# One carried-rows step over four PSUM banks in place of two over two, with new order tables

## The reference, cut to what matters

```python
u = layernorm(x)
zxbcdt = u @ W_in.T                       # z0 512, x0 512, (512 unused), xBC 544, dt 8
dt  = softplus(dt + dt_bias);  A = -exp(A_log)
x, B, C = split(silu(conv4(xBC) + conv_b))       # 8 heads of 64 channels, state of 16
for each token t, each head:                     # the scan
    h = exp(dt_t * A) * h + dt_t * x_t * B_t
    y_t = h . C_t + D * x_t
y = layernorm(y) * ln_gamma + ln_beta
y = sigmoid(y @ W_gate.T + b_gate) * y
x = x + concat(silu(z0) * x0, y) @ W_out.T
# feed-forward
h = layernorm(gelu(layernorm(x) @ ternary(W_fc).T)) ; x = x + h @ ternary(W_proj).T
```

## Time and profile before

| what | value |
|---|---|
| median of three runs | 1161.18 us |
| the profiled execution | 1162.07 us |
| its span (first to last instruction) | 1160.3 us |
| granted TensorE clock, mean | 0.990 |
| PE busy | 1102.1 us, 95% |
| ACT busy | 978.0 us, 84% |
| DVE busy | 969.4 us, 84% |
| POOL busy | 381.9 us, 33% |
| L494, the carried rows | 512 records, 34.2 us |

### The profile page before, as it was taken

How to read it: one execution, slowest core, us unless ns; L and a number is a source line. 1 busy time by engine, 2 the same in 40 slices (tenths; PEclk the granted TensorE clock), 3 DMA queues, 4 the chain that set the end, 5 groups by cost and what they waited for, 6 DMA issues and landing times. The chain is left out here.

```text
span 1160.3 us, 23258 instructions
## 1 busy us (share of the span) xinstructions
PE 1102.1 (95%) x8534; PEld 716.8 (62%) x8534; DVE 969.4 (84%) x1958; ACT 978.0 (84%) x1694; POOL 381.9 (33%) x500
## 2 busy tenths in 40 slices
PE   3789999999999999999999999999999999999995
PEld 1455756576675666666576675756667566757663
DVE  5999999788788898878979898788889889586654
ACT  5787789989888999989798898789888987888765
POOL 1122315341532435142340533323342242515431
PEclk9899999999999999999999999999999999999999
DMA  6510222242424325243424324324343142332465
GB/s 197 165 47 20 66 56 40 57 91 56 93 55 82 85 39 116 47 92 74 72 58 89 68 65 92 84 41 92 77 85 76 37 93 55 74 56 55 89 112 127
DMA packets 238978, 89.15 MB, mean 77 GB/s; under 512 B 207761, under 2 KB 235153, under 8 KB 238865
## 3 DMA queue, kind: packets, MB, share of 16 engines
q1 hardware_dynamic: 238864, 87.67, 35.2%
HBM read 24.32 MB, written 8.39 MB: 28 GB/s over the span
## 5 line engine op out<-in xcount | busy, mean ns | idle before, releaser
L359 PE MATMUL bank<-xnT,win 128*128 128x512 f16 (+1 forms) x1248 | 299.5, 386 | 23.3 <-DMA xnT<-hb 20.3
L359 PEld LDWEIGHTS bank<-xnT,win 128*128 128x128 f16 (+1 forms) x1248 | 121.7, 101 | 156.4 <-issue 31.4
L947 DVE SCALAR_TENSOR_TENSOR cv<-bank,cws,cv 128x510 f32<-128x510 f32 (+5 forms) x240 | 177.8, 744 | 8.3 <-ACT tail L676 2.0
L180 ACT ACT_TABLE_LOAD x137 | 175.8, 1283 | 2.4
L359 PE MATMUL bank<-yhl,wg 128*128 128x512 f16 x768 | 171.6, 379 | 0.5 <-DVE yhl L1094 0.4
L1212 POOL TENSOR_TENSOR cat<-sz,cat 128x512 f16<-128x512 f32 x64 | 78.5, 1229 | 277.6 <-ACT cat L784 277.6
L1208 POOL TENSOR_TENSOR caty<-tg,caty 128x512 f16<-128x512 f32 x64 | 85.5, 1343 | 147.8 <-ACT caty L770 147.8
L587 PE MATMUL bank<-wpj,hT 128*128 128x256 f16 x1024 | 122.6, 274 | 10.3 <-DMA hT<-hb 10.2
L359 PEld LDWEIGHTS bank<-yhl,wg 128*128 128x128 f16 x768 | 74.1, 98 | 89.9 <-issue 2.6
L575 PE MATMUL bank<-wfc,x3T 128*128 128x512 f16 x512 | 122.2, 379 | 3.4 <-ACT EM L741 1.5
L587 PEld LDWEIGHTS bank<-wpj,hT 128*128 128x128 f16 x1024 | 99.2, 98 | 32.3 <-issue 11.5
(11 more groups left out here) (146 smaller groups left out, 2056.3 us busy)
## 6 DMA issues: line engine op xcount, KB each, us to landing
x<-in_x SPq DMA_DIRECT2D x32, 512.0 KB, 4.2
out_y<-x SPq DMA_DIRECT2D x15, 512.0 KB, 3.2
crep<-cv SPq DMA_DIRECT2D x128, 32.0 KB, 2.0
hT<-hb SPq DMA_TRANSPOSE x128, 3.2
caty<-in_wg SPq DMA_DIRECT2D x1, 1024.0 KB, 7.2
x<-in_wout SPq DMA_DIRECT2D x1, 1024.0 KB, 7.2
hT<-in_wfc SPq DMA_DIRECT2D x1, 1024.0 KB, 6.8
cat<-in_wpj SPq DMA_DIRECT2D x1, 1024.0 KB, 8.9
```

Source lines behind the costliest of these rows:

```text
L180: self.eng.preload_act_table_set(self.table)
L359: m = eng.matmul(b, lhs(p, k), rhs(q, k), start=(n == 0), stop=(n == len(seq) - 1))
L947: op = eng.scalar_tensor_tensor(cs[0:w, j, 3 - k:T], b[0:w, 0:T - 3 + k], cws[0:w, j, k:k + 1], cs[0:w, j, 3 - k:T], ALU.mult, ALU.add)
```

## The change

`carried` is now one step a block. It takes four banks at once, and for each chunk gives the products of all four head pairs one after the other, each in its own 32 rows of the array and in its own bank: 16 products in one step, 16 steps in the kernel, where there were 32 steps of 8. `own` and `y_rows` find their banks in the one list. Three waits on the carried step's semaphore count to `i` in place of `2 * i`. The products, their operands and their number are the same.

All five order tables are new. `PE_ORDER` has 980 words in place of 996; the others have as many as before, in another order. Line numbers after `PE_ORDER` go down by one or two.

```diff
 PE_ORDER = (
-    "... q747 q712 o56 p44 ... q717 q720 r735 w7 w7 f56 G64 G61 f57 f52 r704 w7 w7 p41 f53 ..."
+    "... G61 G66 q775 r74312 q760 w7 w7 G67 p45 G66 f50 w7 w7 v77 f56 y75 ..."
...
-            def carried(i, half, at0, at1):
-                js = ((2 * half, at0), (2 * half + 1, at1))
-                hold = {j: take(at) for j, at in js}
+            def carried(i, n, *at):
+                hold = [take(b) for b in at]
                 pe.wait_ge(ce, i + 1)
                 pe.wait_ge(s_done, i + 1)
                 for c in range(NCH):
-                    for j, _ in js:
+                    for j in range(4):
                         m = eng.matmul(hold[j][:, chunk(c)], S[32 * j:32 * j + 32, (4 * i + c) % 5, :],
                                        ec[32 * j:32 * j + 32, chunk(c)], start=(c == 0), stop=False,
                                        skip_group_check=True)
                 m.then_inc(car_mm, 1)
-                for j, at in js:
-                    gives(at, y_out, 4 * i + j + 1)
+                for j in range(4):
+                    gives(at[j], y_out, 4 * i + j + 1)
 
             def own(i, n):
                 p, half = UNITS[n]
-                hold = bank["r", i, half]
+                hold = bank["r", i, 0]
                 pe.wait_ge(em, 4 * i + n + 1)
                 for c in (2 * p, 2 * p + 1):
-                    for j in (0, 1):
+                    for j in (2 * half, 2 * half + 1):
                         for e in range(2):
-                            at = (2 * half + j) * P + 64 * e
+                            at = j * P + 64 * e
...
-                act.wait_ge(car_mm, 2 * i)
+                act.wait_ge(car_mm, i)
...
-                                         bank["r", i, half][j % 2][:, :], ALU.mult, ALU.add).then_inc(y_out, 1)
+                                         bank["r", i, 0][j][:, :], ALU.mult, ALU.add).then_inc(y_out, 1)
```

More of the change, by code:

```diff
@@ L497, in carried @@
                 m.then_inc(car_mm, 1)
-                for j, at in js:
-                    gives(at, y_out, 4 * i + j + 1)
+                for j in range(4):
+                    gives(at[j], y_out, 4 * i + j + 1)
             def own(i, n):
                 p, half = UNITS[n]
-                hold = bank["r", i, half]
+                hold = bank["r", i, 0]
                 pe.wait_ge(em, 4 * i + n + 1)
                 for c in (2 * p, 2 * p + 1):
-                    for j in (0, 1):
+                    for j in (2 * half, 2 * half + 1):
                         for e in range(2):
-                            at = (2 * half + j) * P + 64 * e
+                            at = j * P + 64 * e
                             m = eng.matmul(hold[j][64 * e:64 * e + 64, chunk(c)], Xd[:, c, at:at + 64],
-                                           EM[:, c % 2, 4 * (n % 2) + 2 * j + e, :], start=False, stop=True,
+                                           EM[:, c % 2, 4 * (n % 2) + 2 * (j % 2) + e, :], start=False, stop=True,
                                            skip_group_check=True)
@@ L1014, in zero_s @@
             def zero_s(i, n):
-                dve.wait_ge(car_mm, 2 * i)
+                dve.wait_ge(car_mm, i)
                 then(eng.memset(S[:, (4 * i) % 5, :], 0.0))
```

## The result

The changed kernel takes **1157.15 us** (median of 9 runs, 1155.89 to 1158.96); the kernel before takes 1161.18 (9 runs beside them). The ratio is 0.996, 95% interval 0.9947 to 0.9974: 4 to 5 us faster (3 to 6 by the interval). The forecast was 1150, some 11 us faster. The direction was right, the size somewhat over a third of what I had said.

What follows compares the result with a forecast made beforehand. The prediction took PE's work to bound the middle 900 us: 1162.1 − 13.0 saved + 1.5 of new waits = 1150.6, so 1150 us for a median. The forecast case spanned 1145 to 1155, the whole range 1141 to 1165.

Steps and rivals of the forecast that it cites:

- What the change takes from PE: Carried step: one four-bank step takes 1.16 us and the second step of each block goes, saving 13.0 us.
- the 15 that I had set as its limit: Sign of a right forecast: PE's idle time in the middle 900 us stays under 15 us.
- The first rival: Carried step: four row groups do not run together, pairs go one after the other; 1158 us, chance 0.06.
- the first paragraph: What bounds the kernel: PE, busy 887.53 of the middle 900 us, so PE work removed there shortens the span unless waits replace it.
- the whole term of 13.0 us: Carried steps: PE time saved, 9 x 1.05 us for separate blocks plus 6 x 0.6 us for blocks with halves together.
- I take back 1.5 us: PE in the middle: allowance for new waits for banks, an eighth of the 12.5 us idle, bounds nothing to 15.6 us.
- My second rival: Carried steps: one bank wait of 1.04 us in 15 blocks, 15.6 us, against the 13.0 gained; 1164 us, chance 0.12.
- The remaining reordering: Rest of the new order tables: costed at nothing, with a bound of 5 us either way.
- The fourth rival: New tables: waits such as block 3's go and the ends shorten by a few microseconds; 1142 us, chance 0.10.

Runs made afterwards that it cites:

- (2): Changed kernel with its new tables, each four-bank carried step put back as two two-bank steps side by side: 1157.53 us, ratio 0.9963 to the kernel before.
- (1): Kernel before with its own tables, each carried step leaving out the last two of its four chunks, nothing moved: 1163.27 us, ratio 1.0007.
- (5): Kernel before with 14 of the 16 products in every projection step: 1166.02 us, ratio 1.0031.
- (13): Kernel before with 8 of 16 projection and 2 of 4 fc products: 1156.18 us; its companions, ACT work cut 1152.86 us, DVE work cut 1148.73 us.
- (3): Kernel before with its old tables, the two carried steps joined into one four-bank step in ten of sixteen blocks: 1167.15 us, ratio 1.0038.
- tables_four: Changed kernel's steps (four-bank carried step) with all five order tables re-made, words moved and banks renamed: 1191.12 us, ratio 1.0248 to the kernel before.
- tables_two: Kernel before's two two-bank carried steps with tables re-made in the same way, starting from its own: 1188.0 us, ratio 1.0219.

## Why the prediction was right in direction by luck, and wrong in size and cause

*What the change takes from PE: right.* Four row groups run side by side, the step takes 1.17 us for my 1.16, the group 19.7 us for 18.6 (17 to 19 was the range I gave). PE's busy time fell by 10.2 and not 15: the carried group fell by 14.5, and the other groups together grew by 4.3. PE's idle time in the middle, 16.0 us, came out just above the 15 that I had set as its limit. The first rival is out. The rule of the Trainium skill in "TensorE: Matmul & The Clock Gate", section "Part 3: Packing small matmuls — row/col tiling", which I had weighed as 0.3 us more a block, does not show: four row groups of 128 columns cost no more than two did. The skill's figure is for 512 columns, which no run here has for four row groups.

*The failed step is the first paragraph: "in the middle every microsecond of PE work that goes is a microsecond of the span, unless a wait takes its place".* It carried the whole term of 13.0 us, and that term is worth nothing: the new tables take the same time with one step of four banks and with two of two banks, within about 2 us (2). The same saving in the old tables gave nothing (1), 14 us at the projection made the kernel 3.6 us slower (5), and 116 us gave 6 (13). I had read 98.6% busy as "PE sets the end" and 12.5 us of idle time as all the room there was.

So the right direction was luck. The 4 to 5 us come from the term that I had put at nothing, the new order, and not from the one that I had forecast.

Why did the row mislead? In part since PE's busy time can hold waits. PE's group of projection products in the changed kernel:

```profile
L585 PE MATMUL bank<-wpj,hT 128*128 128x256 f16 x1024 | 122.8, 276 | 10.8 <-DMA hT<-hb 10.3 <-ACT ec L724 0.4
```

Each record lasts 276 ns, but 122.8 us over 1024 of them is 120 ns from one to the next: they overlap. So after the last product of a step some 0.15 us go by before PE counts as idle. I counted from start to start, over the usual distance of each form. By that estimate the 900 us in the middle of the kernel before hold some 110 us beyond the products, of which about 80 us are some 800 gaps of 0.06 to 0.3 us, mostly where one step gives way to the next; the view shows 12.5 us. The level depends on what is taken as a form's need: over the fastest step of each kind it is 46 us. How much of it is waiting and how much a cost of changing over I cannot say. When the products went in experiment 1, this sum rose by 7 to 11 us, and in experiment 13 by 70 to 85 us, whichever way it is counted.

The other part is not in any view of one engine: PE, ACT and DVE each do their steps in a written order, and each hands work to the next. Take work from one and it arrives earlier at a step whose input is not earlier. ACT and DVE showed 115 and 124 us to spare, and yet their microseconds are worth more than PE's: some four times as much as measured, about one and a half times by the estimate at the same clock (13).

*"I take back 1.5 us" for waits: near for banks, and blind to the rest.* I looked for waits for banks only. At the carried steps these grew from 1.3 to 3.6 us, 2.3 more for my 1.5. What I did not look for is larger: 3.0 us more for the states `S` in block 0, and 3.4 us for the transfer of `segR` in the middle. Both stand in experiment 2 as well (4.1 and 4.1), so they belong to the new tables and not to the four-bank step. With the old tables the banks alone cost 11.7 us and make the kernel slower (3). But experiment 1 asks for no bank more than before, and gained nothing either: its new waits are small and spread over banks, `EM` and transfers. My second rival, "the gain becomes waits", at 0.12, had it right that the 13 us are taken back, but its place, the banks, was wrong for the changed kernel.

*"The remaining reordering I cost at nothing, with a bound of 5 us either way": the size of the bound was right, the value not.* It is the whole result, 4 to 5 us off. The fourth rival, "the new tables are better as well", named it at 0.10, but on top of the full saving. What in the new tables does it stays open: they are five tables that depend on each other, and a mixture with single tables of before was not run. The gain is not at one place: the last projection product comes 0.9 us earlier in block 0, 2.2 later in block 1, 14.8 earlier in block 5, 1.3 in block 7, 15.9 in block 8 and 5.0 in block f.

*What does set the pace* is shown only in part. No engine by itself, not the transposing transfers of the rest of `h`; with work off the segment path on all three engines 15 us go. That the rest is the order of steps is likely by tables_four and tables_two, but no order better than the new one was found.

## What to carry to other kernels

Where several engines run written orders and are all above 80% busy, the busiest is not the bound by that alone. Before a saving is counted on the span, leave that work out in place (half the products, nothing moved) and time it: here one line would have shown 0 for 14 us. A step that holds more banks at once can need new tables to be harmless, and then the gain has to be split by running the new tables with the old step. And a sum of idle time in front of a step says nothing until it is split by what ended it: half of the 8.1 us here was one wait for an input in block 0.

## What the runs showed of the hardware

- Four row groups of 32 rows and 128 f32 columns, each into its own bank, start 7 ns apart, a new quartet every 0.11 us: 32 records in 1.17 us, where two row groups need as long for 16.
- At the carried step of the kernel before, 14 us taken off PE give 0 and 14 us put on cost 6.
- With PE's work thinned out by a tenth its mean granted clock was 0.963 to 0.976 in ten runs, against 0.986 to 0.994 in the 18 runs of before beside them, and the products that were left took longer (those of `f` 401 ns in the mean for 379).
- A DVE instruction of 0.34 us (`segL`, f16, 128 columns) took 0.63 to 1.36 us in 33 cases of 288, each time with a POOL instruction already under way when it began.
